# A fused attention and expert kernel: another order of work in its first and last turns

## What is computed

```
s: attention branch, three attentions with shared Wq, Wk, Wv
   blocks of 4 tokens times Wc  -> 128 compressed tokens, attention among them
   64 tokens of highest xn @ Ws -> attention among them
   windows of 32 tokens, step 16 -> attention in each, first 512 outputs
   each times its gate, joined @ Wo + bo, halved, + xn / 2, normalised
f: expert branch, 8 heads
   sim  = (xn @ Wq.T) against 2 x 32 keys per head
   top 16 of each half -> 256 sums -> top 16 of the sums
   h    = gelu(xn @ W_down[chosen]) * softmax(chosen)
   f    = sum of h * W_up[chosen]
```

## Time and profile before

| | |
|---|---|
| median of 3 runs | 279.29 us (279.06 to 279.59) |
| the profiled execution, its time | 281.1 us |
| its span, first to last instruction | 279.4 us |
| VectorE busy | 259.9 us, 93% |
| ScalarE busy | 235.6 us, 84% |
| TensorE busy | 237.8 us, 85% |
| GpSimd busy | 226.0 us, 81% |
| mean granted TensorE clock | 0.982 |

### The profile page before, as it was taken

How to read it: one execution, slowest core, us unless ns; L and a number is a source line. 1 busy time by engine, 2 the same in 40 slices (tenths; PEclk the granted TensorE clock), 3 DMA queues, 4 the chain that set the end, 5 groups by cost and what they waited for, 6 DMA issues and landing times.

```text
span 279.4 us, 7039 instructions
## 1 busy us (share of the span) xinstructions
PE 237.8 (85%) x1562; PEld 176.8 (63%) x1562; DVE 259.9 (93%) x1715; ACT 235.6 (84%) x1048; POOL 226.0 (81%) x344
## 2 busy tenths in 40 slices
PE   7899689797889888978898889888988898879891
PEld 7456243575577667766776577657765776568690
DVE  5899999969999999999999999999999999995885
ACT  2554766868989999899999999999999999996853
POOL 7889701447688899989898989898989898989672
PEclk9999999979999999999999999999999999997997
DMA  7920000000000000010001000100010001000102
GB/s 179 279 74 1 2 0 0 2 1 0 5 0 0 5 0 1 13 31 0 2 3 40 1 0 5 39 0 5 0 39 4 1 0 41 1 1 4 38 1 77
DMA packets 11228, 6.23 MB, mean 22 GB/s; under 512 B 1457, under 2 KB 10674, under 8 KB 11186
## 3 DMA queue, kind: packets, MB, share of 16 engines
q1 hardware_dynamic: 9858, 5.12, 6.9%
q10 hardware_dynamic: 1328, 0.66, 1.1%
HBM read 3.67 MB, written 2.10 MB: 21 GB/s over the span
## 4 chain that ended last, share of the span: by engine, by line
PE 32%; ACT 32%; POOL 19%; issue 13%; DVE 3%; POOLq 0%; ACTq 0%; DVEq 0%
ACT prob L837 6%; PE scratch L1640 4%; PE sim L1548 4%; ACT p_win L936 3%; POOL past L485 3%; POOL squareT L500 3%; ACT gap L759 3%; PE t_bank L1566 3%; ACT away L971 3%; PE s_bank L1742 3%; PE s_bank L1736 2%; ACT spare L856 2%; PE s_bank L1531 2%; ACT sideT L747 2%; ACT side L729 2%
## 5 line engine op out<-in xcount | busy, mean ns | idle before, releaser
L1194 DVE MAX8 top<-rest 128x8 f32<-128x40 f32 x512 | 57.2, 184 | 0.1
L1144 DVE MAX8 top<-sim 128x8 f32<-128x32 f32 x496 | 54.0, 181 | 2.0 <-PE sim L1548 1.9
L837 ACT ACTIVATE prob<-drop 128x50 f32<-128x50 f32 x224 | 51.5, 255 | 0.0
L837 ACT ACTIVATION_READ_ACCUMULATOR prob<-drop 128x1 f32 x224 | 47.1, 212 | 0.0
L500 POOL TENSOR_TENSOR squareT<-sideT 100x512 bf16<-100x512 bf16 x31 | 32.3, 1041 | 6.7 <-ACT sideT L747 6.6
L513 POOL TENSOR_TENSOR wgt<-prob,rden 128x400 f32<-128x400 f32 x30 | 25.7, 855 | 11.8 <-DVE rden L1136 11.7
L1548 PE MATMUL sim<-sim_w,xT_all 128*128 128x512 f32 x64 | 34.7, 625 | 0.5 <-ACT xT_all L784 0.5
L485 POOL TENSOR_TENSOR past<-gap,last 128x400 f32<-128x400 f32 x31 | 26.8, 863 | 9.8 <-DVE last L1218 9.8
L507 POOL TENSOR_TENSOR drop<-gap,out_by 128x400 f32<-128x400 f32 x30 | 31.0, 1033 | 1.1 <-ACT out_by L736 1.1
L1566 PE MATMUL t_bank<-gaps_of,topT 128*128 128x200 f32 x128 | 29.2, 352 | 1.7 <-ACT topT L752 1.7
L1218 DVE MAX8 last<-slot_gap 128x8 f32<-128x22 f32 x256 | 24.4, 168 | 1.1
(11 more groups left out here) (295 smaller groups left out, 753.1 us busy)
## 6 DMA issues: line engine op xcount, KB each, us to landing
out<-y_sb SPq DMA_DIRECT2D x7, 256.0 KB, 2.3
x_sb<-in_L_attn_hidden_states SPq DMA_DIRECT2D x2, 256.0 KB, 4.0
fwq_sb<-in_L_ffn_Wq ACTq DMA_DIRECT2D x2, 256.0 KB, 5.8
x_sb<-in_L_attn_hidden_states SPq DMA_DIRECT2D x1, 512.0 KB, 5.4
wc_sb<-in_L_attn_Wc SPq DMA_DIRECT2D x1, 256.0 KB
out<-last_y SPq DMA_DIRECT2D x2, 128.0 KB, 1.9
wo_in<-in_L_attn_Wo SPq DMA_DIRECT2D x1, 192.0 KB
keys_sb<-in_L_ffn_keys ACTq DMA_DIRECT2D x1, 128.0 KB, 3.4
```

Source lines behind the costliest of these rows:

```text
L837: last = nc.scalar.activation(prob[d][:, h, :], drop[:, h, :], ACT.Exp, scale=-1.0, accum_out=den[d][:, h:h + 1])
L1144: last = nc.vector.max(top[n % 3][:, v, 0:8], sim_bank[n % 2][:, bass.ts(v, KEYS)])
L1194: last = nc.vector.max(top[n % 3][:, v, 8:16], rest[:, v, :])
```

## The change

No instruction is added or removed; the orders change. In the work before turn 4 TensorE transposes the masks and projects vw before it counts tile 0's places, projects the blocks before tile 1's sides, and issues `scores(5)` right after the chosen tokens; row 0's window scores come before turn 4 instead of in it. ScalarE copies the masks before `out_by_of(0)`. VectorE inverts the gates after `mark_above(3)`. In every first turn of a row VectorE's `maxima` comes after `invert_sums` and `spill_above`. For row 7 the units get another order: blocks in turn 30 in the place of vw, chosen tokens and pairs in turn 31, vw after the turns. In turn 31 tile 31's columns and gaps are made as well, with row 7's scores, and GpSimd finishes the weights of tile 27 before `drop_of(28)` and `square_of(29)`, does `past_of(30)` before `gate_attention(5)`, and leaves `drop_of(29)` and `add_input(5)` to the work after.

```diff
@@ m_unit @@
             if b == 0:
                 k = {U_COMP: U_SEL, U_SEL: U_COMP}.get(k, k)
+            elif b == B - 1:
+                k = {U_COMP: U_KW + 1, U_SEL: U_KW + 2, U_QK: U_KW + 3, U_VW: U_KW + 4}.get(k, k)
@@ GpSimd, turn, j == 3 @@
-                    if b >= 2 and n < TILES - 1:
+                    if b >= 2:
                         add_input(b - 2)
+                else:
+                    past_of(n - 2)
+                    weigh(n - 4)
+                    add_halves(n - 4)
+                    add_quarters(n - 4)
+                    drop_of(n - 3)
+                    square_of(n - 2)
+                    past_of(n - 1)
+                    gate_attention(b - 2)
@@ GpSimd, after the turns @@
-            past_of(TILES - 2)
+            drop_of(TILES - 3)
             add_input(B - 3)
-            drop_of(TILES - 3)
             square_of(TILES - 2)
@@ ScalarE, turn, j == 2 @@
                     exps(n - 3)
-                    unit(b, U_VW, [(vw[:, :], 0, bv_sb, 1.0)])
+                    if b < B - 1:
+                        unit(b, U_VW, [(vw[:, :], 0, bv_sb, 1.0)])
+                    else:
+                        unit(b, U_COMP, [(csT[:, 0:BLOCKS], 0, bc_sb, 1.0)])
@@ ScalarE, turn 31, after take_sides(n - 2) @@
-                    unit(b, U_COMP, [(csT[:, 0:BLOCKS], 0, bc_sb, 1.0)])
+                    take_topT(n)
                     unit(b, U_QK, [(qcs[:, :], 0, bqs_sb, SCALE), (kcs[:, :], CS, bk_sb, 1.0)])
                     exps(n - 3)
+                    take_gaps(n)
@@ ScalarE, before turn 4 @@
+            take_masks()
             out_by_of(0)
-            take_masks()
@@ ScalarE, after the turns @@
-            take_topT(TILES - 1)
             out_by_of(TILES - 3)
+            side_of(TILES - 2)
+            unit(B - 1, U_VW, [(vw[:, :], 0, bv_sb, 1.0)])
             unit(B - 1, U_V, [(vcs[:, :], 0, bv_sb, 1.0)])
-            take_gaps(TILES - 1)
-            side_of(TILES - 2)
             window_exps(B - 1, range(LAST))
@@ VectorE, before turn 4 @@
                 select_tokens(3)
+                mark_above(3)
                 invert_gates()
-                mark_above(3)
@@ VectorE, turn @@
                 sum_above(n)
+                invert_sums(n - 4)
+                spill_above(n)
                 if j == 0:
                     maxima(b - 1)
-                invert_sums(n - 4)
-                spill_above(n)
...
                 next_8(n, 0)
+                if n == TILES - 1:
+                    next_8(n, 1)
                 gaps_of_pairs(n - 1)
...
-                next_8(n, 1)
+                if n < TILES - 1:
+                    next_8(n, 1)
                 gaps_of_thirds(n - 1)
-                if n < TILES - 1:
-                    last_gaps(n - 1)
+                last_gaps(n - 1)
@@ VectorE, after the turns @@
-            last_gaps(n - 1)
+            late_gelu()
             maxima(b)
-            late_gelu()
@@ TensorE, turn, j == 2 @@
-                    project_window(b, U_VW, wv_sb)
+                    if b < B - 1:
+                        project_window(b, U_VW, wv_sb)
+                    else:
+                        project_blocks(b, range(RATIO))
@@ TensorE, turn 31, after transpose_sides(n - 2) @@
-                    project_blocks(b)
-                    window_scores(b)
                     project_pairs(b)
+                    expert_weights(n - 4)
+                    top_columns(n)
+                    window_scores(b)
+                    pair_gaps(n)
+                    block_scores(b)
                     count_places(n - 2)
-                    expert_weights(n - 4)
@@ TensorE, before turn 4 @@
             pair_gaps(2)
-            count_places(0)
             transpose_masks()
             project_window(0, U_VW, wv_sb)
+            count_places(0)
             count_ranks()
+            project_blocks(0, range(RATIO))
             transpose_sides(1)
-            project_blocks(0)
             project_selected(0)
+            scores(5)
+            project_pairs(0)
             count_places(1)
-            project_pairs(0)
-            scores(5)
+            window_scores(0)
@@ TensorE, after the turns @@
-            top_columns(TILES - 1)
-            block_scores(b)
+            project_window(b, U_VW, wv_sb)
             project_values(b)
-            pair_gaps(TILES - 1)
```

More of the change, by code:

```diff
@@ L635, in turn @@
                     norm2(b - 1)
-                else:
+                elif n < TILES - 1:
                     past_of(n - 2)
@@ L1013, in turn @@
                     exps(n - 3)
-                    unit(b, U_VW, [(vw[:, :], 0, bv_sb, 1.0)])
+                    if b < B - 1:
+                        unit(b, U_VW, [(vw[:, :], 0, bv_sb, 1.0)])
+                    else:
+                        unit(b, U_COMP, [(csT[:, 0:BLOCKS], 0, bc_sb, 1.0)])
+                elif n < TILES - 1:
+                    take_topT(n - 1)
+                    out_by_of(n - 3)
+                    unit(b, U_SEL, [(csT[:, BLOCKS:CS], 0, None, 1.0)])
+                    side_of(n - 2)
+                    take_gaps(n - 1)
+                    norm_attention(b - 1)
+                    take_sides(n - 2)
+                    unit(b, U_COMP, [(csT[:, 0:BLOCKS], 0, bc_sb, 1.0)])
+                    exps(n - 3)
+                    unit(b, U_QK, [(qcs[:, :], 0, bqs_sb, SCALE), (kcs[:, :], CS, bk_sb, 1.0)])
                 else:
@@ L1022, in turn @@
                     take_sides(n - 2)
-                    unit(b, U_COMP, [(csT[:, 0:BLOCKS], 0, bc_sb, 1.0)])
-                    if n == TILES - 1:
-                        unit(b, U_QK, [(qcs[:, :], 0, bqs_sb, SCALE), (kcs[:, :], CS, bk_sb, 1.0)])
+                    take_topT(n)
+                    unit(b, U_QK, [(qcs[:, :], 0, bqs_sb, SCALE), (kcs[:, :], CS, bk_sb, 1.0)])
                     exps(n - 3)
-                    if n < TILES - 1:
-                        unit(b, U_QK, [(qcs[:, :], 0, bqs_sb, SCALE), (kcs[:, :], CS, bk_sb, 1.0)])
+                    take_gaps(n)
             take_queries(0)
@@ L1641, in project_window, with project_blocks @@
                    start=True, stop=True).then_inc(unit_full, 1)
-            def project_blocks(b):
+            def project_blocks(b, parts):
                 o = fill(m_unit(b, U_COMP))
                 rows = xT_all[:, bass.ts(b, L)].rearrange("p (c r) -> p r c", r=RATIO)
-                for r in range(RATIO):
+                for r in parts:
                     last = mm(o[:, 0:BLOCKS], wc_sb[:, r, :], rows[:, r, :], start=(r == 0), stop=(r == RATIO - 1))
@@ L1753, in turn @@
                     top_columns(n - 1)
-                    window_scores(b - 1)
+                    if b >= 2:
+                        window_scores(b - 1)
                     block_scores(b - 1)
@@ L1788, in turn @@
                     count_places(n - 2)
+                elif n < TILES - 1:
+                    top_columns(n - 1)
+                    project_selected(b)
+                    pair_gaps(n - 1)
+                    transpose_sides(n - 2)
+                    project_blocks(b, range(RATIO))
+                    scores(n + 2)
+                    project_pairs(b)
+                    count_places(n - 2)
+                    expert_weights(n - 4)
                 else:
@@ L1793, in turn @@
                     transpose_sides(n - 2)
-                    project_blocks(b)
-                    if n + 2 in tiles:
-                        scores(n + 2)
-                    if n == TILES - 1:
-                        window_scores(b)
-                    project_pairs(b)
+                    project_pairs(b)
+                    expert_weights(n - 4)
+                    top_columns(n)
+                    window_scores(b)
+                    pair_gaps(n)
+                    block_scores(b)
                     count_places(n - 2)
-                    expert_weights(n - 4)
             def transpose_masks():
```

## The result

The changed kernel takes 278.38 us (median of 14 executions, 276.97 to 281.62), the kernel before 279.79 us beside it (14 executions, 279.06 to 281.38). The ratio is 0.9934, 95% interval 0.9912 to 0.9956: faster by about 0.7%, or 1.8 us. Forecast were 274.9 us, a gain of 4.4, and a range of 273.2 to 277.0. The sign was right, the size was not.

What follows compares the result with a forecast made beforehand. A ring through GpSimd, ScalarE and TensorE, not VectorE, was taken to bound the middle rows, leaving both ends. Head 2.4 and tail 2.0 us off the profiled 281.1 gave 276.7, less 1.8 for the median: 274.9, range 273.2 to 277.0.

Steps and rivals of the forecast that it cites:

- rival 1: Head and tail: the low clock stays, taking 1.2 us and 0.6 of the gain; gain 2.6, 276.7 us; chance 0.16.
- (g): Tail, turn 31: row 7's scores at 256.8 us instead of 258.96, 2.1 earlier, with gaps at full clock.
- (a): Before turn 4: masks' copy ahead of `out_by_of(0)` spares the ranks a wait; 0.45 us, between 0 and 0.76.
- (b): Head: TensorE's new order from `project_selected(0)` takes 4.57 us, so `top_columns(3)` ends near 59.7.
- (c): Head, from `top_columns(3)` to ScalarE's `gap(3)`: it starts at 61.8 instead of 64.24, 2.4 us earlier.
- (d): Row 1 and after: the head's lead lasts, everything 2.4 us earlier if each engine leads by at least 2.4.
- (e): Rows: `maxima` behind `invert_sums` and `spill_above` is worth 0, between 0 and 0.33 us for each of six rows.
- (f): Turn 30: `project_blocks(7)`, 1.9 us, in place of vw's product costs nothing; unhidden it would be 1.4.
- (h): After row 7's scores: last `side` at 261.0 instead of 263.01; tail gain 2.0 us, bounds 1.2 and 2.5.
- 2: Rows follow VectorE after all: the maxima's order frees 0.33 us in each of six, 2.0 more, 272.9; chance 0.10.
- 3: Row 1: the head's lead is lost to an engine with less lead; only the tail's gain left, 277.3; chance 0.10.
- 4: Rows 1 to 6: low-clock stretches fall on TensorE's pieces, making the kernel slower, 284.5 us; chance 0.03.

Runs made afterwards that it cites:

- filled kernel: Kernel before with 19 small unused matmuls where TensorE idles: 278.86 us; the changed kernel with 11 such matmuls: 277.23 us.
- a2_after: The changed kernel again, unfilled and with no further edit: 279.08 us, 0.9966 of the kernel before.
- c5_no_maxima: The changed kernel with VectorE's maxima back ahead of `invert_sums` and `spill_above`, measured once more: 278.23 us.
- v1_less_vectore: Changed kernel with 11 small unused matmuls where TensorE idles, leaving out seven of eight VectorE maxima of tile 31's second half: 276.68 us.
- c3_tail: Kernel before with only the edits of turns 30, 31 and after, maxima in their old place: 278.14 us, ratio 0.9952.

## Why the prediction was wrong

**The step that failed is the one from the profiled execution to the median.** The forecast summed 4.4 us in an execution of 281.1 us, noted that it stood 1.8 above the median, and took the same 4.4 from the median. But the sum held 1.2 us at the head and 0.6 at the tail for the low clock (its own rival 1), 1.8 together, exactly what this execution was above the median. A middling execution of before pays less for the low clock: the median of before is 279.79, its filled kernel takes 278.86, so 0.9. What an execution hasn't paid it can't get back. With the 1.8 taken out, the same sum gives 2.6 at full clock. Measured are 1.63.

**Which term of the 2.6 was too large.** At the head it is the clock's share. 1.2 us is what the stretch would cost in the new order, as rival 1 says; in the old order it cost 1.7, from `gap(2)` to `gap(3)` (12.85 for 11.16). So the head's 2.4 came out nearly whole, 2.3, but with 1.7 of clock and 0.6 of change where the sum has 1.2 and 1.2. At the tail 1.4 was forecast at full clock and 0.8 to 1.0 found; the wait for VectorE under (g) and the long `past` (0.26) are missing from it.

**Added up:** 4.4 forecast; less 1.0 by which the sum at full clock was too large; less 0.9, the part of the 1.8 that a middling execution of before doesn't pay; less 1.15 that the changed kernel pays itself (278.38 for 277.23 filled). That leaves 1.4, which is 279.79 - 278.38. The terms come from batches on different chips and are good to about 0.2.

**The second miss is that the low clock moved.** It is rival 1's mechanism, given 0.16. I put its place at the old ones. The fillings, `a2_after` and `c5_no_maxima` show the new one, turn 5, where TensorE idles in new pieces. There it cost 0.2, 1.3 and 1.7 us in the three traces that have it, and 20 of 35 executions of the changed kernel lie above 277.6. I had looked for idle time that the edits fill and not for idle time that they make further on. That TensorE then waits in turn 5 for engines that had gained less could have been seen by walking on from `gap(3)`.

The Trainium skill says that the clock's monitor is free-running, so that the point where the clock changes at a kernel's start varies from run to run (TensorE: Matmul & The Clock Gate, in What's actually happening, not in the section that the prediction named). The traces agree, and show it far from the start as well: the kernel before has its first dip from 57 us in one and from 52 in the other; the changed one has it from 67 us in two, and none in the third. In all nine traces without filling, of five kernels, six have a dip between 50 and 75 us and three have none.

**Point by point, in the profile.** (a) The masks' order: 0.45 forecast, 0.44 found from `gap(2)` and 0.64 by the medians of two chips, within its bounds. (b), (c) `gap(3)` at 61.8: 61.86. Right, with some luck in the last tenths: that execution has the earliest `gap(2)` of all, and the eleven other traces with this head have 61.88 to 62.39. The clock share, 1.2: 1.7. (d) The lead lasts: 2.4 us at `gap(3)`, 2.4 at the maxima of row 6. Right. (e) Worth nothing in the rows: period 28.15, with the maxima in either place. Right. (f) Hidden, with 0.44 us to spare. Right. (g) Row 7's scores at 256.8 less the head's lead, 254.4: they came at 255.15, 0.75 late. The term left out is VectorE's `gaps_of_thirds(30)`: `top_columns(31)` may not overwrite t_bank before it, and in turn 31 it stands behind 16 maxima. I had counted only GpSimd's quarters in front of the columns. TensorE stands 0.39 us for it, and 0.4 of the 0.75 was there already when the weights ahead of the columns were done. `v1_less_vectore` shows the wait: 0.72 us less of VectorE's work, 0.55 us less time (0.5 counted from `gap(2)` to the end of the span). (h) The last `side` at 261.0 less 2.4, 258.6: 258.93. In all 3.9 us in the profiled executions for 4.4.

**The rivals.** 2 and 3 fall: the rows kept their period, and the lead was not lost where the clock was full. 4, low clock in the rows, happened in one turn and not in six. It took back part of the gain.

**Open.** I have no trace of the unfilled kernel before at full clock. But its seven executions with the highest mean clock (278.91) and the filled one (278.86) agree, and `c3_tail`, which has the head of before without fillings, takes 11.25 us from `gap(2)` to `gap(3)` for the filled 11.16, with a low-clock stretch from 53 to 57 us that its idle time before tile 1's count takes up. So the fillings do not distort the head by more than 0.1 us. What decides in which executions turn 5 is hit, and for how long, was not found.

## What to carry to other kernels

Ask first what makes the profiled execution longer than the median, and take that out of the sum before anything else: here the two low-clock stretches were more than the whole difference, and a gain that removes them is a gain of that one execution. Compare traces from the last common point ahead of the edit and not by their absolute times: 10.5 us from `gap(2)` to `gap(3)` held to 0.02 in twelve traces whose `gap(3)` varied by 0.5. When an edit takes a wait from one engine, follow the others until their next wait, because idle time of TensorE moves with them and can bring the low clock somewhere else, as in turn 5 here. Where executions of one program spread, a few products without a use in TensorE's idle places are a cheap way to tell the clock from everything else, and they may stay in: the filled kernel with `add_input` later is the fastest found that does all the work, 276.97 us for 279.93.

## What the hardware did that I had not expected

VectorE's `past` reads two tensors in SBUF. Started 0.08 us after GpSimd's `add_input`, it ended 0.4 us after it and took 1.62 us. With GpSimd idle it took 0.58. The square that GpSimd started meanwhile took 1.37 instead of 1.04 us. The Trainium skill has a rule for this (GPSIMD Engine Reference, Specifications): the two engines share SBUF interfaces, with contention for VectorE's instructions with two SBUF inputs; the traces agree: 1.62 or 1.63 us in eight profiles with `add_input` started just ahead of it, 1.76 in the one where `past` started 0.06 us ahead of `add_input`, and 0.58 in the two where GpSimd stands idle. In all nine it ended 0.4 us after `add_input`. It wasn't asked of this change, though the change put the two side by side.

The median of the changed kernel was 278.38, 279.08 and 277.40 us in three batches of twelve to fourteen executions, 1.7 us apart, as much as the change is worth. With five small products in turn 5, which took up about 1.2 us of TensorE's idle time there (0.65, 0.44 and 0.53 us became 0.15, 0.23 and none), the six executions lay within 0.5 us, for 2.4 us among the eleven of the unfilled kernel beside them, and the median was 277.19.
